# The experts' products of a transformer block on half the rows of TensorE each: two tiles side by side in three passes, one transpose

## What is computed

```python
x2  = einsum('bct,bcd->bdt', x, W[condition])      # cond2: mixes the 64 channels of a batch
gate = softmax(x2 @ gate_W.T);  weights, sel = top_k(gate, 2);  weights /= sum(weights)
h   = einsum('td,erd->ter', x2, A) * (w_dense * 2.0)   # 8 experts of rank 8: 64 values a token
out = x2 @ W_base.T + einsum('ter,eor->to', h, B)      # the experts' product: [64] by [64, 1024]
x   = x + out
```

## Time and profile before

| | us |
|---|---|
| median of three runs | 876.0 |
| the profiled execution | 876.56 |
| its span, first to last instruction | 874.7 |
| TensorE busy (PE) | 854.1 |
| vector engine busy (DVE) | 467.1 |
| GpSimd busy (POOL) | 450.0 |
| ScalarE busy (ACT) | 221.4 |

### The profile page before, as it was taken

The page is one execution under the profiler, slowest core; times in us unless marked ns, Lnnn a source line. Parts: engine busy times, 40 slices in busy tenths (PEclk is TensorE's granted clock), DMA queues, the critical chain, the costliest instruction groups (busy, mean ns, idle before and its releaser), DMA issues.

```text
span 874.7 us, 24616 instructions
## 1 busy us (share of the span) xinstructions
PE 854.1 (98%) x10866; PEld 741.9 (85%) x10866; DVE 467.1 (53%) x898; ACT 221.4 (25%) x377; POOL 450.0 (51%) x346
## 2 busy tenths in 40 slices
PE   3999999999999999999999999999999999999998
PEld 2899999988888888887777777777779999999998
DVE  7555651122522222238887777888854755545444
ACT  4445552100000000013132333333334322211220
POOL 3344555302367555649978888877746422102220
PEclk9999999999999999999999999999999999999999
DMA  3788877413354322255534454545437211222211
GB/s 95 177 207 220 208 186 196 162 60 127 109 183 129 82 74 73 50 166 154 142 129 149 135 176 165 173 163 173 151 123 234 96 59 57 83 97 97 98 49 49
DMA packets 97339, 114.90 MB, mean 131 GB/s; under 512 B 44112, under 2 KB 66896, under 8 KB 97232
## 3 DMA queue, kind: packets, MB, share of 16 engines
q1 hardware_dynamic: 94240, 112.29, 43.1%
q10 hardware_dynamic: 2480, 0.51, 0.3%
q0 software_dynamic: 512, 0.53, 0.2%
HBM read 80.16 MB, written 33.13 MB: 130 GB/s over the span
## 4 chain that ended last, share of the span: by engine, by line
PE 93%; SPq 3%; DMA 2%; DVE 1%; issue 0%; ACT 0%
PE ps L988 25%; PE ps L1275 21%; PE ps L1597 15%; PE ps L649 8%; PE ps L1625 5%; PE ps L952 5%; PE ps L660 4%; PE ps L1231 3%; PE ps L1211 3%; PE ps L1507 2%; SPq L606 2%; DMA toep<-kpad 2%; PE ps L1642 1%; PE ps L1641 1%; DMA kpad<-ksb 1%
## 5 line engine op out<-in xcount | busy, mean ns | idle before, releaser
L1597 PE MATMUL ps<-wb_hi,xf 128*128 128x424 f32 x440 | 127.0, 356 | 0.0
L988 PE MATMUL ps<-y_hi,w_hi 128*128 128x512 f32 x320 | 125.1, 391 | 0.0
L988 PE MATMUL ps<-y_hi,w_lo 128*128 128x512 f32 x320 | 124.5, 389 | 0.0
L988 PE MATMUL ps<-y_lo,w_hi 128*128 128x512 f32 x320 | 124.5, 389 | 0.0
L1573 POOL TENSOR_TENSOR xf<-xs,xf 128x512 fp32r<-128x512 f32 x32 | 42.1, 1347 | 124.8 <-DVE xs L1561 124.8
L1275 PE MATMUL ps<-y_hi 128*128 128x512 f32 x256 | 102.9, 402 | 0.0
L1275 PE MATMUL ps<-y_hi,y_lo 128*128 128x512 f32 x256 | 100.2, 391 | 0.0
L1275 PE MATMUL ps<-y_lo,y_hi 128*128 128x512 f32 x256 | 100.1, 391 | 0.0
L649 PE MATMUL ps<-xc,toep 64*128 64x192 f32 (+4 forms) x1088 | 97.1, 330 | 2.5 <-DMA toep<-kpad 2.4
L649 PEld LDWEIGHTS ps<-xc,toep 64*128 64x128 f32 x1088 | 91.2, 187 | 6.0 <-issue 3.8
L1597 PEld LDWEIGHTS ps<-wb_hi,xf 128*128 128x128 f32 x440 | 82.7, 188 | 2.3
(11 more groups left out here) (190 smaller groups left out, 1624.3 us busy)
## 6 DMA issues: line engine op xcount, KB each, us to landing
toep<-kpad SPq DMA_DIRECT2D x124, 136.0 KB
xc<-in_dram SPq DMA_DIRECT2D x32, 256.0 KB, 4.4
q_rows<-rf SPq DMA_DIRECT2D x32, 256.0 KB, 2.8
q<-q_rows SPq DMA_DIRECT2D x16, 512.0 KB, 3.9
xr<-in_dram SPq DMA_DIRECT2D x16, 512.0 KB, 4.4
x_scratch<-xr SPq DMA_DIRECT2D x16, 512.0 KB, 3.0
x<-x_scratch SPq DMA_DIRECT2D x16, 512.0 KB, 4.3
out_dram<-x SPq DMA_DIRECT2D x15, 512.0 KB, 2.9
```

Source lines behind the costliest of these rows:

```text
L988: mm = pe.matmul(kq_bank(n), w[a][:, j, :], yt[b][:, j, g * 512:(g + 1) * 512], start=(j == 0 and a + b == 0), stop=(j == NJ - 1 and a == 1))
L1597: mm = pe.matmul(dst[:, PLAIN:], xf(i, idx, a)[:, t, :], wb(c, idx, t), start=(start and t == 0 and a + c == 0), stop=(t == 3 and a == 1), ...
```

## The change

- `hw` holds h of both tiles side by side (tile 0 in columns 0 to 63, tile 1 in 64 to 127), each once. One transpose turns both: tile 0 comes to lie on partitions 0 to 63, tile 1 on 64 to 127.
- ScalarE writes the high part of it to `ht[0]`, the vector engine the low part to `ht[1]`, each [128, 128].
- `experts(pe, half, banks, fresh)` makes one half of the output for both tiles: three passes, in each one matmul with tile 0's 64 rows and one with tile 1's 64 rows, with the same 64 rows of B (on their own half of the partitions), into two banks. That is six matmuls of 64 rows, 128 columns and 512 moving columns for a half, twelve a pair. The product of low part by low part, which the form before had in it, is not made.
- The right halves stand before the sixth product (D_BANK and `other_bank`), the left ones behind it (C_BANK and `sum_bank`). The sixth product now starts C_BANK (`start=True`).
- `pe_x` is counted up twice a pair; the addition of C_BANK waits for the second count as well.

```diff
-        hw = block_at("hw", 2, [P, 2, 2, NH])
-        ht = place("ht", 2 * BLK + 4 * NH, [2 * NH, 2, P], F32R)
+        hw = block_at("hw", 2, [P, 2, NH])
+        ht = [place(f"ht_{n}", 2 * BLK + at, [2 * NH, P], F32R) for n, at in (("hi", 2 * NH), ("lo", 2 * NH + P))]
...
         def turn_h(pe, i):
             pe.wait_ge(v_h, i + 1)
-            for k in range(2):
-                mm = pe.transpose(turned_h(i)[:, k * P:(k + 1) * P], hw[:, k, :, :].rearrange("p a n -> p (a n)"), C("ident"))
-            mm.then_inc(pe_ht, 1)
-
-        def experts(pe, k, half, dst, start):
+            pe.transpose(turned_h(i), hw[:].rearrange("p k n -> p (k n)"), C("ident")).then_inc(pe_ht, 1)
+
+        def experts(pe, half, banks, fresh):
+
             cols = slice(half * HALF_OUT, (half + 1) * HALF_OUT)
-            pe.matmul(dst, ht[:, k, :], bexp_hi[:, cols], start=start, stop=False, skip_group_check=not start)
-            return pe.matmul(dst, ht[:, k, :], bexp_lo[:, cols], start=False, stop=True, skip_group_check=not start)
+            for a, c in PASSES:
+                for k in range(2):
+                    rows = slice(k * NH, (k + 1) * NH)
+                    start = fresh[k] and a + c == 0
+                    mm = pe.matmul(banks[k], ht[a][rows, :], (bexp_hi, bexp_lo)[c][rows, cols],
+                                   start=start, stop=(a == 1), skip_group_check=not fresh[k])
+            mm.then_inc(pe_x, 1)
...
-                experts(pe, 0, 0, C_BANK, start=True)
-                experts(pe, 0, 1, D_BANK, start=False)
-                experts(pe, 1, 1, other_bank(i), start=True).then_inc(pe_x, 1)
-                product(pe, i, 5, C_BANK)
+                experts(pe, 1, (D_BANK, other_bank(i)), (False, True))
+                product(pe, i, 5, C_BANK, start=True)
                 added(pe, 8 * i + 4)
-                mm = experts(pe, 1, 0, sum_bank(i), start=False)
+                experts(pe, 0, (C_BANK, sum_bank(i)), (False, False))
                 if i + 1 < NP:
                     product(pe, i, 6, sum_bank(i))
                 else:
-                    mm.then_inc(pe_x, 1)
                     for n in range(2):
                         last_product(pe, i, n)
...
-                act.activation(ht[:].rearrange("p k n -> p (k n)"), turned_h(i), ACT.Copy).then_inc(a_hthi, 1)
+                act.activation(ht[0][:], turned_h(i), ACT.Copy).then_inc(a_hthi, 1)
...
-            for copy in range(2):
-                ins = v.tensor_tensor(hw[:, :, copy, :].rearrange("p k (e r) -> p k e r", r=RANK),
-                                      gsum[:, :, NE:NPROJ].rearrange("p k (e r) -> p k e r", r=RANK),
-                                      gt[:, 0, :, :].unsqueeze(3).to_broadcast([P, 2, NE, RANK]), ALU.mult)
-            ins.then_inc(v_h, 1)
+            v.tensor_tensor(hw[:].rearrange("p k (e r) -> p k e r", r=RANK),
+                            gsum[:, :, NE:NPROJ].rearrange("p k (e r) -> p k e r", r=RANK),
+                            gt[:, 0, :, :].unsqueeze(3).to_broadcast([P, 2, NE, RANK]), ALU.mult).then_inc(v_h, 1)
...
-                v.tensor_tensor(ht[NH:, :, :].rearrange("p k n -> p (k n)"), turned_h(i)[NH:, :],
-                                ht[NH:, :, :].rearrange("p k n -> p (k n)").bitcast(F32), ALU.subtract).then_inc(v_htlo, 1)
+                v.tensor_tensor(ht[1][:], turned_h(i), ht[0][:].bitcast(F32), ALU.subtract).then_inc(v_htlo, 1)
...
-                v.wait_ge(pe_x, i + 1)
+                v.wait_ge(pe_x, 2 * i + 1)
                 v.wait_ge(v_plain, 2 * i + 2)
                 add_again(v, i, 4, 1, 1, other_bank(i))
                 add_again(v, i, 3, 0, 1, D_BANK)
                 v.wait_ge(pe_p, 7 * i + 6)
+                v.wait_ge(pe_x, 2 * i + 2)
                 add_again(v, i, 1, 0, 0, C_BANK)
                 if i + 1 < NP:
                     v.wait_ge(pe_p, 7 * i + 7)
                     add_to(v, i, 1, 0, sum_bank(i))
                 else:
-                    v.wait_ge(pe_x, NP + 1)
                     add_to(v, i, 1, 0, sum_bank(i))
```

More of the change, by code:

```diff
@@ L1629, in turned_h @@
         def turned_h(i):
-            return other_bank(i)[:, 0:2 * P]
+            return other_bank(i)[:, 0:P]
         def turn_h(pe, i):
             pe.wait_ge(v_h, i + 1)
-            for k in range(2):
-                mm = pe.transpose(turned_h(i)[:, k * P:(k + 1) * P], hw[:, k, :, :].rearrange("p a n -> p (a n)"), C("ident"))
-            mm.then_inc(pe_ht, 1)
-        def experts(pe, k, half, dst, start):
+            pe.transpose(turned_h(i), hw[:].rearrange("p k n -> p (k n)"), C("ident")).then_inc(pe_ht, 1)
+        def experts(pe, half, banks, fresh):
             cols = slice(half * HALF_OUT, (half + 1) * HALF_OUT)
-            pe.matmul(dst, ht[:, k, :], bexp_hi[:, cols], start=start, stop=False, skip_group_check=not start)
-            return pe.matmul(dst, ht[:, k, :], bexp_lo[:, cols], start=False, stop=True, skip_group_check=not start)
+            for a, c in PASSES:
[5 more added lines that the diff above has]
+            mm.then_inc(pe_x, 1)
         def added(pe, n):
```

## The result

The change made the kernel slower by a little: 880.65 us median of 13 runs (877.10 to 883.06) against 877.19 for the kernel before in as many (874.11 to 879.78). The ratio is 1.0035, with a 95% interval of 1.0019 to 1.0051, that is +3.1 us (1.7 to 4.5). The forecast was +1.8 us and 877.8 us, with a range of 875.1 to 879.4.

What follows compares the result with a forecast made beforehand. The prediction took PE (TensorE) to bound the kernel, busy 854.1 of 874.7 us. Per pair +0.80 - 0.46 - 0.11 = +0.23 us, over eight pairs +1.8, from a median of 876.0 gave 877.8 us, range 875.1 to 879.4.

Steps and rivals of the forecast that it cites:

- "slower": Whole kernel: the measured time comes out slower by more than a measurement can tell from no change, 2.6 us; chance 0.26.
- The sum: TensorE, per pair of tiles: +0.80 - 0.46 - 0.11 = +0.23 us; over eight pairs +1.8 us.
- (a): Experts' matmuls: six couples at 0.23 us each replace eight full-array matmuls, -0.46 us a pair, bounds -0.58 and -0.40.
- rival C: Experts' blocks: a couple costs more than one step, its matmuls all 0.23 apart; at 0.27 a couple 3.8 us slower; chance 0.06.
- (b): Transposes ahead of the fifth product's end: one of two goes, -0.11 us a pair.
- (c): Around the experts' blocks: four switches between 128*128 and 64*128 a pair at 0.20 us, +0.80, bounds 0.58 and 0.88.
- A': Experts' blocks: the way into 64*128 costs only 0.09 us, giving +0.01 us a pair, 876.1 us; chance 0.16.
- B: Experts' blocks: switching between whole and halved rows costs nothing, -0.57 us a pair, 871.4 us; chance 0.08.
- The sign "0.34 more from the end of the fifth product to the start of the seventh": Changed profile, mid-kernel: TensorE was to take 0.34 us more over this stretch than before.
- (d): Right halves, sixth product, left halves: the new order leaves TensorE's work the same and only moves additions; counted as nothing.
- (e): Ahead of the experts' blocks: no new wait, 0.6 us to spare for h's low part, 1.5 for the fourth addition.
- (f): End of the kernel: last addition moves with PE, left tile's store still 2.5 us ahead of the last; counted as nothing.

Runs made afterwards that it cites:

- the third experiment: The changed kernel with the two loops of `experts` exchanged, tile 0's three passes ahead of tile 1's; ratio 1.0032, 879.14 us against 876.96 for the kernel before.
- the second experiment: The changed kernel with the right halves moved behind the sixth product too, two changes of form a pair; ratio 1.0006 to the kernel before, 877.71 us against 876.96.
- first experiment: The kernel before, full-array form, with only the order of the change on TensorE; ratio 1.000, 876.75 us against 876.96.

## Why the prediction was wrong

The direction of the mean was right and its chance for "slower" (0.26) too small; the time, 880.65, fell outside the range. Two steps failed. The sum put the products' own steps at nothing, without a reason, and they cost 0.12 us a pair. And the whole forecast was laid on a median of three runs, with no room in the range for how far that median could be off. The signs by which the prediction would have called itself wrong, a change of form under 0.12 or over 0.24 us and a couple that is not one step, did not come; the miss lay in a term that none of them watched. Point by point:

- **(a) Couples: right.** 0.23 us each, from the row of the same type and width; rival C is out. But the reason given in the third experiment's expectation, that they must be issued side by side, was wrong.
- **(b) Transpose: right**, 0.11.
- **(c) Changes of form: right**, and it is the term that decides. 0.20 in and 0.20 out in the trace, and 0.42 for two by the second experiment. A' (a cheap way in, 0.09) and B (none) are out. One reading behind it was off: 706.42 is the start of the mixing's last matmul, its last group of four starts at 706.40, so the way out of the mixing is 0.22 and not 0.20; and of the way into it 0.05 more lie in the first group of four, which takes 0.11 us where the others take 0.06. The sum used neither. The sign "0.34 more from the end of the fifth product to the start of the seventh" came out as 0.27 (4.39 us, 713.16 to 717.55, against 4.12): half of the last change, 0.10, lies inside the seventh product's first matmul, behind that stretch. The Trainium skill's rule that a change of tiling mode drains TensorE ("TensorEngine Tiling (Array Packing)", Key Properties) holds here with that price.
- **(d) Order, (e) waits, (f) end: right.** The order alone gives 1.000. The low part of h is ready at 712.24 (711.96 and 0.28 in the fence below) for a block at 713.25; the first of the three additions from 713.95, the fourth of the pair, is over long before 716.66. In the view of waits TensorE waits for nothing from 676 us on, in either kernel. From the last addition to the end it is 2.9 us as before.

The timeline of the vector engine in the changed kernel, which answers to the earlier trace rows:

```profile
711.96 0.28 DVE L1794 TENSOR_TENSOR ht_lo<-ps,ht_hi 128x128 fp32r<-128x128 f32 x1
...
713.95 2.00 DVE L1767 TENSOR_TENSOR x<-ps,x 128x424 f32<-128x424 f32 x3
717.72 0.69 DVE L1767 TENSOR_TENSOR x<-ps,x 128x512 f32<-128x512 f32 x1 [1.76 <-PE ps L1597]
```

- **The sum: one term was missing.** It took the products' own steps as given. They are not: from the second pair on the fourth to seventh product go at 0.193 or 0.194 a matmul in the changed kernel and at 0.190 before. That is some 0.15 us a pair, and with 0.02 more in the first three products and 0.05 less in the plain ones it makes the 0.12, 0.9 us in all (2.7 in the trace, 1.8 in the sum). +0.23 becomes +0.35. That is a third of the loss. The bounds of the sum (-0.9 to +3.4) held the 2.7 us that the trace shows, because the price of a change of form had been given room upward; the room was in the wrong term.
- **The median it stood on.** The forecast was laid on 876.0, the median of three runs; thirteen gave 877.2. Of the 2.85 us between forecast and result (880.65 less 877.8) 1.2 are this, and 0.9 the missing term; no term explains the remaining 0.8. Laid on 877.19, the same sum gives 879.0 with a range of 876.3 to 880.6, and the result would have stood just above its upper end. Runs of one and the same program lie 5.7 us apart. The part ahead of the change alone differs: the first mixing starts at 653.09 in the profiled execution of before and at 654.50 in that of after, at 652.03 in the third experiment's, with the same instructions up to there. The difference between 2.7 us in the trace and 3.1 in the ratio is well inside the interval.

What sets the steps of the products is open. What the traces show is this:

- They come in two kinds, 0.190 and 0.193, that hold for a whole product. The longer kind isn't new: in the kernel before the first two products of each pair have it, the third to the seventh don't.
- It doesn't need the form 64*128. The mixing's new place alone, all in the full-array form, gives it to the fifth product, and in the changed kernel the fifth product of the first pair has it, ahead of which no experts' block has run. The order of the experts' products alone, in the full-array form, changes nothing (first experiment), and in the versions with the blocks behind the mixing, with three changes of form a pair, the fourth to the seventh product have 0.190.
- The number of transposes isn't it either. From the second pair on, and where the mixing stands ahead of the fourth product, the fifth has 0.190 behind two transposes and 0.193 behind one; where the mixing stands behind the fifth, it is the other way about (0.193 behind two, 0.190 behind one). In the last pair, which has no mixing, both kinds occur behind one transpose and behind two.

Address, contention and phase weren't told apart.

## What to carry to other kernels

Where TensorE is the bound, price a switch between whole and divided array like an instruction: 0.20 us each way here, nearly one 512-column matmul. A divided form must save more than the way in and the way out at each place where it stands, so gather its work in one block, best beside work that is divided already. By these prices three couples in each of two blocks lose 0.34 us here (0.80 less 0.46), six in one block save 0.06, which no time showed, and six beside the mixing, with one change more, save 0.26. And in a run of thousands of matmuls a step that is 2% longer is a term of the sum of its own: compare steps of untouched instructions before and after.

## What the runs showed of the hardware that I had not expected

- Matmuls ran out of the order of the source: with tile 0's three passes written first and then tile 1's, the fourth ran beside the first, and the block took the same three steps. The Trainium skill ("TensorE: Matmul & The Clock Gate", Packing small matmuls) has matmuls start and end strictly in program order; for matmuls on different rows this trace shows otherwise, if the order of the source is the program order there.
- The same matmuls (128x424, fp32r, the same operands and banks) go at 0.190 or at 0.193 us a step, a whole product long, and in the kernels here a transpose more, or another place of the mixing, switched them.
- A wait of 2.8 us of TensorE was followed by a granted clock of 0.50 (1.2 GHz) in the next 3.5 us (TensorE was busy 0.39 of the 3.00 us before); the sixth and seventh product around it took 9.75 us, and 4.67 in the later pairs of the same kernel, so the stall cost almost twice its length.
